# TensorE runs constant products at four waits of a decoder layer's group loop

## The reference

```python
# block 1, on x of (32, 128, 128)
xn1 = layernorm(x);  pot = xn1 @ w_pot + b_pot          # two scalars a row
x = x + bk_core_diag(V, gamma) @ w_bk + b_bk             # continued fractions along the sequence
q, k, v = (layernorm(x) @ w_qkv + b_qkv)                 # 8 heads of 64
x = x + hebbian_scan(q, k, v, gamma) @ w_out + b_out     # decayed linear attention, causal
x = x + gelu(layernorm(x) @ w_ff1 + b_ff1) @ w_ff2 + b_ff2
# block 2: cross attention, 16 heads of 8, over ctx_1024 of (32, 128, 128)
probs = softmax((xq * 8**-0.5) @ xk.T + mask * -100.0)
out = (probs @ xv) @ Wo.T + bo
# block 3: 8 experts, the best two of each row, 128 -> 512 -> 128 with gelu
```

## Time and profile before

| | |
|---|---|
| median of 3 runs | 801.77 us (800.95 to 807.67) |
| the profiled execution | 798.83 us |
| its span, first to last instruction | 797.0 us |
| granted TensorE clock, mean over the span | 0.901 |
| PE busy | 670.7 us, 84% |
| DVE busy | 512.8 us, 64% |
| ACT busy | 400.8 us, 50% |
| POOL busy | 320.8 us, 40% |

### The profile page before, as it was taken

One profiled execution on the slowest core, in us unless ns is written; L12 is line 12 of the kernel. 1 busy time (PEld: TensorE's weight loads), 2 busy tenths in 40 slices (PEclk: granted clock), 3 DMA queues, 4 the chain that ended last, 5 costly groups with the idle time before them and its releaser, 6 DMA issues.

```text
span 797.0 us, 19859 instructions
## 1 busy us (share of the span) xinstructions
PE 670.7 (84%) x6190; PEld 502.2 (63%) x6190; DVE 512.8 (64%) x1733; ACT 400.8 (50%) x855; POOL 320.8 (40%) x463
## 2 busy tenths in 40 slices
PE   9789979888997987988888899798576999999920
PEld 9565636745854763764674585476353799999920
DVE  4687477767667768667676766766546355555535
ACT  0312555464474374465547347446240477777726
POOL 6104560363264165057136326405404255544535
PEclk8579997999998999899899899899575999999965
DMA  8500000000000000000000000000022222222144
GB/s 295 195 15 1 22 21 3 2 24 17 0 20 20 0 20 20 0 1 33 7 0 20 20 0 20 20 0 7 22 107 68 70 69 73 71 66 74 57 157 181
DMA packets 26058, 36.23 MB, mean 45 GB/s; under 512 B 7302, under 2 KB 18311, under 8 KB 25736
## 3 DMA queue, kind: packets, MB, share of 16 engines
q1 hardware_dynamic: 20582, 22.72, 9.2%
q0 software_dynamic: 4576, 9.53, 3.4%
q10 hardware_dynamic: 850, 3.38, 1.3%
HBM read 23.99 MB, written 12.63 MB: 46 GB/s over the span
## 4 chain that ended last, share of the span: by engine, by line
PE 53%; DVE 20%; issue 12%; POOL 5%; ACT 4%; DMA 2%; SPq 1%; another core or an unknown queue 1%; DVEq 1%; ACTq 0%; POOLq 0%
PE bank L1543 8%; PE bank L1858 8%; PE bank L1868 8%; PE bank L1708 4%; POOL rstd L737 3%; PE bank L1579 3%; PE bank L1677 3%; PE bank L1695 3%; DVE stats L1044 2%; ACT mix L555 2%; PE bank L1627 2%; PE bank L1716 2%; DVE negmax L1169 2%; PE bank L1635 2%; PE bank L1730 1%
## 5 line engine op out<-in xcount | busy, mean ns | idle before, releaser
L734 POOL TENSOR_SCALAR vare<-mv 128x1 f32<-128x1 f32 (+1 forms) x108 | 23.9, 221 | 267.2 <-DVE mv L1049 266.9
L856 POOL DMA_INDIRECT expert_out<-xa,v_sb x71 | 68.3, 962 | 77.2 <-issue 47.2
L675 ACT ACTIVATE hT<-bank,qT 128x128 f32<-128x128 f32 x284 | 81.0, 368 | 36.3 <-issue 19.8
L1169 DVE TENSOR_REDUCE negmax<-bank 128x4 f32<-128x512 f32 x128 | 80.2, 684 | 21.8 <-PE bank L1677 12.6
L555 ACT ACTIVATE mix<-bank 128x512 f32<-128x512 f32 x128 | 66.1, 603 | 36.9 <-PE bank L1695 36.6
L779 POOL DMA_INDIRECT expert_in<-xb_rows,slot_u x72 | 71.9, 999 | 31.1 <-issue 18.5
L1868 PE MATMUL bank<-w_t,hT 128*128 x568 | 75.5, 276 | 1.1 <-DVE xa L1389 0.5
L1858 PE MATMUL bank<-xnT,qT 128*128 128x128 f32 x568 | 75.1, 275 | 0.4 <-issue 0.4
L1868 PEld LDWEIGHTS bank<-w_t,hT 128*128 128x128 f32 x568 | 69.1, 192 | 2.0 <-issue 1.8
L737 POOL TENSOR_TENSOR rstd<-vare,minus_half 128x1 f32<-128x1 f32 (+1 forms) x108 | 66.5, 615 | 9.6 <-POOL vare L734 1.2
L1858 PEld LDWEIGHTS bank<-xnT,qT 128*128 128x128 f32 x568 | 69.0, 192 | 0.6 <-issue 0.6
(11 more groups left out here) (300 smaller groups left out, 1490.9 us busy)
## 6 DMA issues: line engine op xcount, KB each, us to landing
v_sb<-expert_in SPq DMA_DIRECT2D x71, 66.0 KB
w_t<-in_w_t ACTq DMA_DIRECT2D x1, 2064.0 KB, 7.5
x_all<-in_x SPq DMA_DIRECT2D x4, 512.0 KB, 7.7
xT_all<-in_xT SPq DMA_DIRECT2D x4, 512.0 KB, 8.3
ctxT<-in_ctxT SPq DMA_DIRECT2D x8, 256.0 KB, 2.9
w_t<-in_w_t SPq DMA_DIRECT2D x1, 2048.0 KB, 7.5
x_all<-expert_out SPq DMA_DIRECT2D x4, 512.0 KB, 10.0
mix<-expert_out SPq DMA_DIRECT2D x3, 512.0 KB, 7.4
```

What stands on the lines that cost most here:

```text
L675: ins = nc.scalar.activation(hx[j % 2][:, c, :], bank[2 + j % 2][:, c * P:(c + 1) * P], ACT.Gelu, bias=w1c[j % 2][:, FF + c:FF + c + 1])
L856: nc.gpsimd.indirect_dma_start(ys[:, :], bass.IndirectOffsetOnAxis(ap=tag[j % ROWS][:, HOME - P:HOME - P + 1].bitcast(U32), axis=0), ysb[j ...
L1169: nc.vector.tensor_reduce(negmax[t % 2][:, i, 28:28 + XC], b[:, :].rearrange("p (c n) -> p c n", c=XC), AX.X, ALU.max, negate=True).then_i ...
```

## The change

Eighteen constant products are added to a group. `place_queries` takes its four banks ahead of the wait for `qf` instead of behind it, and six products go between the two. `key_scores` of tile 0 gets six behind its takes and ahead of the wait for `mT0`. The output projection gets two between the take of its first bank and the wait for `cxT` (not in the last group), and the last tile of the transposed norm gets four of 128 columns (not in the last group).

```diff
             def place_queries(g):
+                b = [take(pe, g, f"qs{c}") for c in range(XC)]
+                spin(b[0], 6)
                 drained(pe, g, "qf")
-                b = [take(pe, g, f"qs{c}") for c in range(XC)]
                 for part, rows in enumerate((high, low)):
...
                 def key_scores(t):
                     b = [take(pe, g, f"st{t}i{i}") for i in range(4)]
+                    if t == 0:
+                        spin(b[0], 6)
                     drained(pe, g, f"mT{t}")
...
                 if not last:
                     scores(g, 3)
+                first = take(pe, g, "xo0")
+                if not last:
+                    spin(first, 2)
                 drained(pe, g, "cxT")
                 for t in range(T):
-                    b = take(pe, g, f"xo{t}")
+                    b = take(pe, g, f"xo{t}") if t else first
...
-                    turn(g, "xh3T", LN3, g + 1, xn)
+                    turn(g, "xh3T", LN3, g + 1, xn, (0, 0, 0, 4))
```

## The result

The changed kernel takes 811.98 us (median of 13 runs, 809.99 to 815.53) against 800.74 us of the kernel before (13 runs), a ratio of 1.0134 with a 95% interval of 1.0112 to 1.0156. It is slower by 1.3%. The profiled execution has a span of 810.2 us, 13.2 us more than before.

What follows compares the result with a forecast made beforehand. PE was taken to bound the group loop, through its waits and its clock. The terms 4.5 + 9.1 + 0 + 0 + 3.9 - 11.7 = +5.8 us gave 807 us, range 795 to 821 us.

Steps and rivals of the forecast that it cites:

- A change within 1%: Whole kernel: measured time within 794 to 810 us, chance 0.47, against 0.15 faster and 0.38 slower.
- The products stand behind the waits: Both sets of six: bank takes ahead of them are the waits, so products start only when the wait is over.
- The distance named for it: First placed query to first key score: 9.05 us before, 10.3 us with DVE's idle time full, 11.6 us with it moved.
- Key scores, 9.1 us: Six products before the first key scores: all 1.29 us added in each of seven groups, 9.1 us.
- Placed queries, 4.5 us: Six products before the placed queries: 0.65 us a group, middle of 0 and 1.29 us; 4.5 us over seven.
- The clock, 11.7 of 17.5 us: Stretch behind the key scores: gain of 17.5 us if the clock never falls; two thirds, 11.7 us, chosen.
- Output projection and last norm, nothing: Two products ahead of the projection and four small ones in the last norm: covered by waits, cost nothing.
- Last group, 3.9 us: First two sets at low clock: 2.5 us for queries, 1.3 us for key scores, together 3.9 us (2.6 to 5.0).
- the hole takes up the queries' set: Rival: DVE's idle time before tile 1's maxima absorbs the queries' products, clock stays high; -4.5 us, 797 us, chance 0.22.
- the clock is worth more: Rival: stretch behind the key scores without a fall is 20.94 us, gain 24.6 us; -11.6 us, 790 us, chance 0.10.
- the clock falls as before: Rival: no clock gain in the loop; +17.5 us, up to +23.2 us, 819 to 825 us, chance 0.20.
- the products fill the waits: Rival: products cost nothing and only the clock gain is left; -17.5 us, 784 us, chance 0.05.

Runs made afterwards that it cites:

- the second trace of the same loop: Trace of the changed kernel without the two sets of six products in the last group; 802.41 us, ratio 1.0043 to the kernel before.
- the two other traces of this chip without products there: Changed kernel without last-group sets of six (802.41 us), and that kernel with its loop sets moved ahead of the waits (782.52 us).
- the two small edits: Kernel before plus only two products ahead of the output projection and four in the last norm's wait; 769.22 us, ratio 1.0007, second chip.
- the late row transfers: Kernel before with GpSimd's row transfers, mask cast and ff residual sum started after tile 1's key scores; 768.80 and 769.79 us, second chip.
- six products inside each wait: Changed kernel, both sets of six moved ahead of the bank takes that wait, none in the last group; 782.52 us, ratio 0.9794 to kernel before.

## Why the prediction was right or wrong

**The time and the sign.** 807 us was forecast, 811.98 us measured, inside the range of 795 to 821 us. A change within 1% was held the likeliest; it came out 0.3% beyond that bound. The sum had +5.8 us, and the medians differ by 11.2 us. The terms beside what the traces show: the two large sets 13.6 us put, 18.0 us found; the clock -11.7 us put, -14.7 us found; the last group 3.9 us put, 6.9 us found between these two traces. The first two errors go against each other (+4.4 and -3.0 us), and the third adds 3.0 us; so the sum hides a part of what its terms had wrong.

**The products stand behind the waits.** Right, and it is the cause. It could be read from the order of the rows and the bank table alone: the take of `qs3` is the wait for `qf`, and the take of `st0i0` is the wait for `negmax`. The distance named for it was counted wrongly: the queries' set stands ahead of the first placed query, so from there to the key scores a hole that moves along gives 9.05 + 1.29 = 10.3 us and not 11.6 us, and a hole that takes the delay up leaves 9.05 us and not 10.3 us. The trace has 10.81 us. Counted from the end of the queries' wait, where both sets are in it, 11.6 us stand against 1.38 + 10.81 = 12.19 us.

**Key scores, 9.1 us.** Nearly right. Alone the set adds 10.35 - 9.05 = 1.30 us in the third group, and 8.5 us in the sum of the seven. A set takes 1.39 us in the traces and not 1.29 us, since there is 0.1 us between its last product and what follows.

**Placed queries, 4.5 us.** Right alone, wrong in company. Alone the hole takes up 0.57 of 1.20 us, which leaves 7 x 0.63 = 4.4 us. With both sets the distance to the key scores grows by 10.82 - 9.48 = 1.34 us in the mean of the groups, which is all of the 1.39 us of the key scores' set but 0.05 us: almost nothing of the queries' set is taken up. (In the third group the growth is 1.76 us, since the distance before was at its shortest there.) The step that failed is the middle between 0 and 1.29 us for the queries' set: it was taken for the set by itself, and beside the other set the whole of it is paid, the upper bound of 9.1 us and not 4.5 us. Over the loop, the two sets cost 3.3 us net plus what the clock gave, 14.7 us (below), so 18.0 us, where 4.5 + 9.1 = 13.6 us had been put. On the second chip, where no clock comes back, the loop is 18.4 us longer.

**The clock, 11.7 of 17.5 us.** The full price was nearly right: 22.33 us without a fall was measured, 21.96 us had been worked out, so the upper end was 14.7 us rather than 17.5 us (first group 25.45, second 22.76, the five others 122.8 us together, less 22.33 us each: 3.1 + 0.4 + 11.2 = 14.7 us). In the second group the two slow pieces were 0.80 us longer, but the stretch only 0.43 us. The share was wrong: not two thirds of the groups but all seven kept it in this trace, and six of seven in the second trace of the same loop. The second error is larger than the first: some 14.7 us came back where 11.7 us had been put. The Trainium skill's sentence on the released throttle ("TensorE: Matmul & The Clock Gate", section "What's actually happening") was the better guide for the loop on this chip (1.00 over the whole loop); on the second chip the clock is at 1.00 over the whole loop without any of the products, and they have nothing to release.

**Output projection and last norm, nothing.** Right. The start of the projection moves by 0.44 us and its wait shrinks; over the loop the waits of PE for `hT` there fall from 5.1 to 2.7 us and those for the normed tile from 3.8 to 2.5 us. The run with both alone has a ratio of 1.0007, on the second chip.

**Last group, 3.9 us.** Probably too small; how much is open. It is 6.9 us against the trace of the kernel before, 2.9 and 4.1 us against the two other traces of this chip without products there, and 5 to 10 us by the medians; on the second chip it is 64.6 us against 58.9 us. Both sets ran at 1.2 GHz and took 2.64 and 2.67 us. The 1.3 us put for the second took off a gain of the clock behind it. What the products do to the clock behind them is within its scatter: from the key scores to the projection it is 24.75 us at 0.64 with them, and without them 22.93 us at 0.72 in the trace of the kernel before and 26.50 and 26.48 us at 0.50 in the two others.

**The rivals.** That the hole takes up the queries' set held for half of it and only alone. That the clock is worth more is out by the 22.33 us. That the clock falls as before is out on this chip. That the products fill the waits did not happen, but it showed what the change could have been: 782.5 us, when 784 us had been worked out for it. The nearness is in part luck: 17.5 us had been put on the clock alone, where 14.7 us came from it and 3.4 us from shorter distances to the key scores.

## What to carry to other kernels

Work that is to fill a wait must stand ahead of every wait that ends as late: look at which bank, buffer or counter each `take` stands for, not at the name in the last wait. A product that keeps the clock up is worth what the slow stretch behind it costs, here 2.1 us a group, and costs its whole length as soon as it stands in the path, here 1.4 us. Before filling a wait, find out whether the wait belongs to the kernel or to the chip of the profile: here the wait for `negmax`, up to 2.86 us in the trace of the kernel before, did not exist on a second chip.

## What was not expected of the hardware

Two chips gave the same program 799 us and 768 us. In the traces the difference in the loop is the hole of 1.35 to 2.8 us ahead of the maxima, and the fall of the clock that follows it: 9.05 us and more against 7.61 us from the queries to the key scores, and 0.95 against 1.00 over the loop. On the first chip DVE waits there for products that PE's records show as finished: recorded until 247.70 us, read from 249.17 us on. On the second, in the kernel with the two small edits, it is 238.98 and 239.04 us:

```profile
238.31 0.67 PE L1677 MATMUL bank<-kr,qr 32*128 32x128 f32 x16
...
239.04 2.47 DVE L1169 TENSOR_REDUCE negmax<-bank 128x4 f32<-128x512 f32 x4
```

What makes the hole is open, and so is whether it belongs to a chip for good or to its state at the time.

On the chip with the hole it does not go away when the work around it moves. From the queries to the key scores the changed kernel has 10.81 us there and 9.00 us on the other chip, 1.8 us apart. Without the large sets it is 9.05 to 10.49 us (the kernel before, mean 9.48 us) and 7.61 us (the kernels with the two small edits and with the late row transfers), 1.9 us apart. So the extra time moves along with the work and stays what it was. With six products inside each wait the two chips are only 0.2 us apart (9.00 and 8.80 us): the time that PE loses in the hole is then nearly all filled.
